# Depthwise taps over whole images, and another order on three engines, in a conv mixer

## The reference

```python
h = _layernorm(x, n1_g, n1_b)
p = h @ w_in + b_in                                    # 96 -> 192 channels
local = conv_general_dilated(p, k_conv, 'SAME', feature_group_count=192)   # 3x3, each channel by itself
lr, rl = _ema_scan(local, axis=2), _ema_scan(local, axis=2, reverse=True)
tb, bt = _ema_scan(local, axis=1), _ema_scan(local, axis=1, reverse=True)
mixed = 0.25 * (lr + rl + tb + bt) + local
mixed = _layernorm(mixed, on_g, on_b)
x = x + (mixed @ w_out + b_out)
```

## Time and profile before

| | |
|---|---|
| median of 3 runs | 1159.32 us |
| the profiled execution, and its span | 1162.63 us, 1160.7 us |
| busy over the span: TensorE, VectorE, ScalarE, GpSimd | 89%, 59%, 50%, 43% |
| all 256 halves of taps 1 to 8 (L1059) | 75.3 us busy, 362 ns each |
| first and last such instruction | 220.1 us, 330.9 us |

### The profile page before, as it was taken

One profiled execution on the slowest core, in us unless ns is written; L12 is line 12 of the kernel. 1 busy time (PEld: TensorE's weight loads), 2 busy tenths in 40 slices (PEclk: granted clock), 3 DMA queues, 4 the chain that ended last, 5 costly groups with the idle time before them and its releaser, 6 DMA issues. The chain is left out here.

```text
span 1160.7 us, 29149 instructions
## 1 busy us (share of the span) xinstructions
PE 1036.5 (89%) x11331; PEld 683.3 (59%) x11331; DVE 685.7 (59%) x2018; ACT 582.6 (50%) x1335; POOL 502.8 (43%) x675
## 2 busy tenths in 40 slices
PE   5999989688879799999999997888898888899998
PEld 2677755466645467767776763464545444466665
DVE  3899834589966455656665653674557556343423
ACT  1676633256643276665666663544344322365553
POOL 4766555455547345555554546153001000354542
PEclk9999999789989999999999998887999999899999
DMA  6400000000000000000000000000000000000000
GB/s 126 92 4 2 3 1 2 1 1 3 2 2 1 1 1 1 2 1 3 1 1 1 2 1 1 1 2 1 1 2 2 2 1 1 1 9 16 9 16 15
DMA packets 28391, 9.72 MB, mean 8 GB/s; under 512 B 26529, under 2 KB 28256, under 8 KB 28256
## 3 DMA queue, kind: packets, MB, share of 16 engines
q1 hardware_dynamic: 25232, 6.95, 2.9%
q10 hardware_dynamic: 3024, 0.92, 0.4%
HBM read 6.29 MB, written 1.57 MB: 7 GB/s over the span
## 5 line engine op out<-in xcount | busy, mean ns | idle before, releaser
L1109 POOL TENSOR_TENSOR fa_e<-fa_e,fa_rc 128x1024 f32<-128x1024 f32 x64 | 120.7, 1895 | 142.2 <-DVE fa_rc L1332 142.1
L1266 ACT ACTIVATE fa_e<-bank,fa_nm 128x256 f32<-128x256 f32 x256 | 118.9, 500 | 0.0
L137 PE MATMUL bank<-hT,e_w 96*64 96x512 f32 x384 | 90.4, 606 | 0.0
L2117 ACT ACTIVATE ex_G<-bank,e_b 128x512 f32<-128x512 f32 x96 | 64.5, 687 | 49.3 <-PE bank L137 46.6
L164 POOL TENSOR_TENSOR ln_v<-MV,eps 128x2 f32<-128x2 f32 (+3 forms) x81 | 16.7, 206 | 162.9 <-DVE MV L201 91.2
L2189 DVE SCALAR_TENSOR_TENSOR X<-bank,ex_L,X 128x96 f32<-128x96 f32 x128 | 31.8, 311 | 91.5 <-PE bank L137 84.9
L1326 DVE TENSOR_REDUCE fa_nm<-bank 128x4 f32<-128x1024 f32 x64 | 75.5, 1220 | 14.7 <-PE bank L1135 14.7
L2020 POOL TENSOR_TENSOR ex_tmp<-e_b,ex_L 128x384 f32<-128x384 f32 x8 | 6.7, 835 | 169.2 <-DVE ex_L L2177 169.2
L1921 DVE TENSOR_REDUCE ca_z<-bank 128x2 f32<-128x256 f32 x96 | 48.9, 551 | 49.5 <-PE bank L1648 49.5
L1839 ACT ACTIVATE ca_e<-bank 128x768 f32<-128x768 f32 x48 | 38.9, 811 | 77.4 <-PE bank L1648 77.4
L137 PEld LDWEIGHTS bank<-e_w,ex_G 128*64 128x64 f32 x1536 | 67.2, 137 | 17.2 <-issue 10.5
(11 more groups left out here) (251 smaller groups left out, 2488.4 us busy)
## 6 DMA issues: line engine op xcount, KB each, us to landing
out_tokens<-X SPq DMA_DIRECT2D x8, 192.0 KB, 2.1
X<-in_x SPq DMA_DIRECT2D x14, 96.0 KB, 3.5
e_w<-in_L_ffn_w SPq DMA_DIRECT2D x2, 576.0 KB
bias0r<-in_L_conv_rpb_table ACTq DMA_DIRECT2D x16, 24.0 KB
m0w<-in_L_conv_mlp_w SPq DMA_DIRECT2D x2, 144.0 KB
m1w<-in_L_conv_w SPq DMA_DIRECT2D x2, 144.0 KB
f_w<-in_L_ffn_W SPq DMA_DIRECT2D x2, 142.5 KB
mixer<-in_mixer SPq DMA_DIRECT2D x1, 256.0 KB
```

Source lines behind the costliest of these rows:

```text
L137: last = pe.matmul(out[columns], weights[:, columns], moving, **flags)
L1109: pool.tensor_tensor(e, e, r.broadcast_to([P, 4, TOK]), ALU.mult).then_inc(s["nrm"], 1)
L1266: last = act.activation(E[v % 4][:, i, c, :], bank[b + i][:, c * TOK:(c + 1) * TOK], ACT.Exp, bias=NM[v % 4][:, i, c:c + 1], accum_out=SU[ ...
L2117: act.activation(G[e % 2][:, j, :], bank[(KH * e + j) % NB][:], ACT.Gelu, bias=k.eb1[:, e, j:j + 1]).then_inc(s["gelu"], 1)
```

## The change

Taps of VectorE are one instruction over the whole image, 256 elements per partition, each waiting for the tap before it. The small operations stand one by one between the taps: the residual behind tap 0, one own statistic behind each of taps 1 and 2, both aggregates behind tap 3, one statistic of the mixed rows behind each of taps 5 and 6, both aggregates behind tap 7. On TensorE, tokens and back move ahead of conv_t, and widen moves from behind taps to in front of mix. On ScalarE, hT and zt move ahead of loc, and widened moves from the end of the turn to right behind loc. GpSimd's list stays.

The diff, cut to its core:

```diff
@@ TensorE
                 for n in range(IMAGES + 3):
                     slot = n % 2
-                    if 1 <= n <= IMAGES:
-                        conv_t(n - 1, 1 - slot)
                     if n + 1 < IMAGES:
                         tokens(n + 1, 1 - slot)
                     if n >= 3:
                         back(n - 3)
                     if 1 <= n <= IMAGES:
+                        conv_t(n - 1, 1 - slot)
+                    if n + 1 < IMAGES:
+                        widen(n + 1, 1 - slot)
+                    if 1 <= n <= IMAGES:
                         mix(n - 1)
                     if n < IMAGES:
                         taps(n, slot)
-                    if n + 1 < IMAGES:
-                        widen(n + 1, 1 - slot)
                     if n >= 3:
                         out(n - 3)
...
@@ VectorE
+                def own_stats(n, t):
+                    if t == 0:
+                        dve.wait_ge(s["x"], n + 1)
+                        after(dve, s["mv"], n)
+                    dve.bn_stats(k.stats[:, t, :], k.X[:, 2 * n + t, None, :]).then_inc(s["bn"], 1)
...
+                def mixed_stats(n, t):
+                    if t == 0:
+                        dve.wait_ge(s["mix"], n + 1)
+                        after(dve, s["va2"], 2 * n)
+                    dve.bn_stats(st2[:, t, :], mixed[n % 2][:, t * CI:(t + 1) * CI]).then_inc(s["bn2"], 1)
...
+                def tap(n, i):
+                    slot = n % 2
+                    o = acc[slot][:].rearrange("p (i c) -> p i c", c=SIDE)
+                    y, x = divmod(i, 3)
+                    src = grid[slot][:, 0, y:y + SIDE, x:x + SIDE]
+                    kk = k.kconv[:, 0, i:i + 1]
+                    if i == 0:
+                        dve.wait_ge(s["p"], n + 1)
+                        after(dve, s["ct"], n - 1)
+                        dve.tensor_scalar(o, src, kk, None, ALU.mult).then_inc(s["conv"], 1)
+                    else:
+                        dve.wait_ge(s["conv"], TAPS * n + i)
+                        dve.scalar_tensor_tensor(out=o, in0=src, scalar=kk, in1=o, op0=ALU.mult, op1=ALU.add).then_inc(s["conv"], 1)
```

More of the change, by code:

```diff
@@ L1037, in residual @@
                     add_new(dve, k, s, n, 2, bank[6][:, 0:2 * C].rearrange("p (t c) -> p t c", t=2))
[L1039 to L1059, removed]
@@ L1061, in _, with own_moments @@
[L1061 to L1062 removed]
+                def own_stats(n, t):
[3 more added lines that the diff above has]
+                    dve.bn_stats(k.stats[:, t, :], k.X[:, 2 * n + t, None, :]).then_inc(s["bn"], 1)
+                def own_moments(n):
+                    alone(dve, k)
+                    dve.wait_ge(s["bn"], 2 * n + 2)
+                    for t in range(2):
+                        last = dve.bn_aggr(k.MV[:, 2 * n + t, :], k.stats[:, t, :])
+                    last.then_inc(s["mv"], 1)
@@ new lines, in mixed_stats, with mixed_moments @@
+                def mixed_stats(n, t):
[3 more added lines that the diff above has]
+                    dve.bn_stats(st2[:, t, :], mixed[n % 2][:, t * CI:(t + 1) * CI]).then_inc(s["bn2"], 1)
+                def mixed_moments(n):
+                    alone(dve, k)
+                    dve.wait_ge(s["bn2"], 2 * n + 2)
+                    for t in range(2):
+                        last = dve.bn_aggr(ag2[:, t, :], st2[:, t, :])
+                    last.then_inc(s["ag2"], 1)
@@ new lines, in _ @@
+                for n in range(IMAGES):
+                    tap(n, 0)
+                    if n >= 4:
+                        residual(n - 4)
+                    tap(n, 1)
+                    if n >= 4:
+                        own_stats(n - 4, 0)
+                    tap(n, 2)
+                    if n >= 4:
+                        own_stats(n - 4, 1)
+                    tap(n, 3)
+                    if n >= 4:
+                        own_moments(n - 4)
+                    tap(n, 4)
+                    tap(n, 5)
+                    if n >= 1:
+                        mixed_stats(n - 1, 0)
+                    tap(n, 6)
+                    if n >= 1:
+                        mixed_stats(n - 1, 1)
+                    tap(n, 7)
+                    if n >= 1:
+                        mixed_moments(n - 1)
+                    tap(n, 8)
@@ L1063, in _ @@
                 for n in range(IMAGES - 4, IMAGES):
                     if n == IMAGES - 3:
-                        norm2(IMAGES - 1)
+                        for t in range(2):
+                            mixed_stats(IMAGES - 1, t)
+                        mixed_moments(IMAGES - 1)
                     residual(n)
-                    statistics(dve, k, s, n, 2)
+                    for t in range(2):
+                        own_stats(n, t)
+                    own_moments(n)
 def full_attention(k, bank):
```

23 lines of the change are left out of this document (6 added, 17 removed).

## The result

The changed kernel takes 1142.84 us (median of 4 runs, 1141.52 to 1143.34); the kernel before, run beside it, 1160.37 (4 runs, 1157.04 to 1163.28). The ratio is 0.985, with a 95% interval of 0.982 to 0.988. The forecast of 1141.5 is 1.3 us off and its likeliest case held. Two terms of the sum were nevertheless mis-sized, and one small row had been misread. That the forecast came so near is in part luck: the sum gave 1144.8 us for the profiled execution, which took 1142.76, and the 3.3 us taken off for the median were not there this time (profiled 1142.76, median 1142.84).

The account below looks back on a forecast made before the run. VectorE was taken as the bound from image 7, a loop through widen before, TensorE next; savings of 8.5, 7.6 and 1.7 made 17.8 us, so 1144.8 for the profiled execution and 1141.5 as median, range 1135 to 1151.

Parts of the forecast that it names:

- likeliest case: Whole kernel: the forecast of 1141.5 us, with 1137 to 1146 as its own range and a chance of 0.62.
- VectorE's part: VectorE's turn in the mixer: 5.12 us an image from whole, interleaved taps, 5.4 with 0.3 for GpSimd.
- GpSimd's hold: Mixer: GpSimd's wide operations delay taps, 0.3 us an image; as rival 0.9, VectorE the bound, 1147 us, chance 0.14.
- images 7 to 14: Mixer, eight images at TensorE's turn of 5.64 us in place of 53.59 us together: 8.5 us saved.
- it waited 0.1: TensorE in front of mix: waits 0.2 us for loc in the new order, where before it waited 0.1.
- The count of 5.44: TensorE's work for one mixer image, summed from start to start without waits: 5.44 us, unchanged by moving instructions.
- the rival in which GpSimd is shut out: Mixer: GpSimd's operations wait for whole taps, its turn becomes 7.8 us and `Y` is late; 1175 us, chance 0.05.
- Images 2 to 6: Mixer, five images at 5.64 us in place of 35.84 together: 7.6 us saved, if the clock stays up.
- Images 0 and 1: Mixer start: image 0 at 5.4 us, image 1 at 8.7 at half clock, together 1.7 us saved.
- Behind the last tap nothing gets shorter: End of the mixer, behind the last tap: no time saved.
- joining and interleaving bring nothing: Rival on VectorE: a whole tap occupies 0.52 us, 6.4 an image; 1152 us, or 1155; chance 0.10.
- the clock did not drop: Rival, TensorE's clock falls in the mixer: 3.6 us missing, 1145 us, or twice that, 1149; chance 0.09.

Follow-up runs that it names:

- loc_first: Changed kernel with back behind conv_t on TensorE and zt behind loc on ScalarE, throughout the mixer; 1141.01 us, ratio 0.983.
- pe_light: Changed kernel with four of the six TensorE matmuls for the taps of the 64 other channels left out; 1136.02 us (1 run).
- second profiles: The kernel before and the changed kernel, each profiled once more unedited; mixer 119.85 and 102.54 us.
- dve_only: VectorE's part of the change alone, TensorE and ScalarE in the order of the kernel before; 1142.64 us, run again 1147.26.
- tail_fix: Changed kernel, but from the last image on conv_t in front of back and loc in front of zt; 1139.91 us, ratio 0.984.
- after_again: The changed kernel run and profiled again, unedited; 1143.21 us, ratio 0.987.
- halved: Changed kernel with every VectorE tap in two halves of 128 elements again; 1153.16 us, ratio 0.995.
- grouped: Changed kernel with whole taps, but VectorE's small operations in three groups as before the change; 1147.05 us, ratio 0.990.

## Why the prediction was right, point by point

**VectorE's part held.** The tap (476 ns, predicted 479), what it occupies (0.40), the turn with GpSimd's hold (5.42, predicted 5.4) and the hold itself (the row at 278.90: 0.32, predicted 0.3) are all as worked out. That the hold is GpSimd's is read from what runs beside it: the row stands beside `X<-X,b_out`, and the same tap of image 14, when GpSimd has no image left to normalise, takes 0.47 us:

```profile
278.82 0.59 POOL L173 TENSOR_TENSOR X<-X,b_out 128x192 f32<-128x192 f32 x1
...
301.95 0.47 DVE L1065 SCALAR_TENSOR_TENSOR cm_acc<-cm_g,k_conv,cm_acc 128x256 f32<-128x256 f32 x1
```

Two small errors about cancel in the turn: the first tap occupies 0.26 us (274.91 to 275.17) where 0.33 was counted, and GpSimd takes 0.1 more, from the pair of taps at 277.09 (1.09 us, and 0.97 in image 14). Taking 0.40 between 0.28 and 0.52 from the two rows of the same operation was the choice that carried the sum.

**TensorE became the bound, as forecast**, at 5.74 us an image where 5.64 was predicted; eight images at 0.1 make the 0.8 us by which images 7 to 14 fell short. The step that failed is the reading that before "it waited 0.1" in front of mix, and that this was for loc. In the trace before, mix at 279.26 starts 0.53 behind back, of which 0.09 to 0.10 is the change from weight tiles of 128 columns to those of 64. It stands wherever such tiles meet: now in front of widen (276.04) and in front of tokens (280.46). The count of 5.44 held neither of them. The first product behind each change is 0.04 to 0.05 longer as well (tokens 0.42 against 0.38, widen 1.08 against 1.03). The wait for loc came to 0.09, not 0.2 (widen to mix takes 1.01, and 0.92 in loc_first, where loc is in time). By starts: tokens 0.26, back 0.44, conv_t 0.65, widen 1.01, mix 1.35, taps 1.30, out 0.76, together 5.77, where the prediction had 0.22, 0.43, 0.62, 0.86 with 0.2 of wait, 1.35, 1.30 and 0.66. The Trainium skill, "TensorEngine Tiling (Array Packing)" (Key Properties), says that a change of tiling mode drains TensorE. The trace agrees in that each such change loses time, 0.09 to 0.10 us; that it is a drain no row shows.

**VectorE waits for mix**, 5.1 us in 13 images, 0.39 each, where 0.5 was predicted (by shape, 233 to 306 us: busy us, mean ns, idle before):

```profile
L1044 DVE BATCH_NORM_STATS2 cm_st<-bank 128x6 f32<-128x192 f32 x26 | 9.4, 360 | 5.1 <-PE bank L137 5.1
```

GpSimd's wait for `cm_ag`, the room that kept `Y` in time, went from 2.43 us an image to 1.18 or 0.52, turn by turn:

```profile
274.70 0.35 POOL L863 TENSOR_TENSOR cm_v<-cm_ag,eps 128x2 f32<-128x2 f32 x1 [1.18 <-DVE cm_ag L1050]
```

`Y` was in time, and the rival in which GpSimd is shut out is refuted, with half a microsecond or more to spare from image 4 on. In images 2 and 3 nothing is to spare, and in pe_light tokens waits 0.79 us for `Y` there (233.93).

**Images 2 to 6 held** (7.8, predicted 7.6), and the clock stayed up as the term assumed. Part of that is luck: images 2 and 3 took 5.38 and 5.35 us, images 4 to 6 5.76 in the mean, and the term had 5.64 for all five.

**Images 0 and 1 were mis-sized**: 4.0 us in place of 1.7. Image 0 took 5.53 us, as priced (5.4); image 1 took 6.32 in place of 8.7. The prediction priced image 1 at half clock throughout; in this profile the clock rose at 225.20, 7.4 us behind the first tap. Between the second profiles the term is 3.1 (14.55 - 11.50), so some 0.9 of the 4.0 is chance in the clock of the kernel before.

**The tail came to 0, but as a sum of two terms that the prediction did not have.** Shorter taps save 1.5 us there (dve_only: 15.31 against 16.83), and 1.9 come back. Of these 0.7 go with the clock, at its lower level from 317.40: the last product with `cm_zT` takes 1.55 us in place of 0.88 (339.46 of before). The other 1.2 are zt in front of loc, with no widen to cover it: the two waits of 0.91, without which tail_fix is 1.36 shorter than after_again, 0.14 of it in that last product (1.41). "Behind the last tap nothing gets shorter" looked at the taps alone; a loop's last turns have other neighbours than its middle, and wanted their own count.

**The rivals.** That joining and interleaving bring nothing is refuted by halved and grouped (their turns are 1.1 and 0.6 us longer than the changed kernel's). GpSimd's hold stayed at 0.3 to 0.4. Between its rise and image 15 the clock did not drop in either profile of the changed kernel.

## What to carry to other kernels

Where two engines are both near the bound, work out each one's own turn without its waits; the gain ends at the second, and an order that fills the second's idle time is worth little while the first is the bound (in images 7 to 14 here 0.3 us alone, and 2.0 to 2.4 behind VectorE's part). A chain of dependent operations on VectorE is shortened by fewer, longer instructions and by an independent one between any two, and the two ways can be measured apart. Count the first and the last turns of a software pipeline by themselves: what covers a moved step in the middle may be missing there, and giving the last turns an order of their own (tail_fix) cost the middle nothing here (27.98 and 45.86 us, after_again 27.98 and 45.87).

## What the runs showed of the hardware

- The rows write a weight tile as rows*columns. A group of products on tiles of 128*128 or 128*96 and one on tiles of 128*64 or 96*64 start 0.09 to 0.10 us further apart than two groups of one kind, in either direction (276.04 and 280.46 of the changed kernel).
- VectorE's taps and GpSimd's operations are longer beside each other. GpSimd's nine operations of an image add up to 4.0 us in before, 4.2 in halved, 4.5 in grouped and 4.8 in the changed kernel (sums of their means). Single ones go by what they meet: the one on line 165 takes 751 ns in the changed kernel, 537 in before, and 522 in grouped, which has whole taps too; `cm_v` takes 351 beside whole taps and 213 in halved:

```profile
L165 POOL TENSOR_TENSOR Y<-X,MV 128x192 f32<-128x192 f32 x11 | 8.3, 751 | 0.0
...
L863 POOL TENSOR_TENSOR cm_v<-cm_ag,eps 128x2 f32<-128x2 f32 x13 | 4.6, 351 | 13.4 <-DVE cm_ag L1050 13.4
```

```profile
L863 POOL TENSOR_TENSOR cm_v<-cm_ag,eps 128x2 f32<-128x2 f32 x11 | 2.3, 213 | 25.3 <-DVE cm_ag L1050 25.3
```

  The first fence is of the changed kernel, the second of halved, all by shape from 233 to 306 us (busy us, mean ns, idle before). In halved the halves lost 0.83 us of a turn, in the changed kernel whole taps some 0.4.
